# Cross-attention of a perceiver block: denominators of a quarter of the queries from the maximum tiles

## Chip, cores and metric

One core of one Trainium2 chip. The metric is device time in microseconds (us) for one execution, the median of several. Engines are called by the profile's names: PE (TensorE matmul), PEld (TensorE weight load), DVE (VectorE), ACT (ScalarE), POOL (GpSimd), SP (SyncE, which issues the DMAs).

## The reference, cut to what matters

```
q = (x @ Wq + bq).reshape(B, N, 16, 32)        # layer-normed x: 512 queries of 512
k = (y @ Wk + bk).reshape(B, M, 16, 32)        # y: 8192 context rows of 384
v = (y @ Wv + bv).reshape(B, M, 16, 32)
scores = einsum('bnhd,bmhd->bhnm', q, k) / sqrt(32)
attn = softmax(scores, axis=-1)                # over 8192 keys
out = einsum('bhnm,bmhd->bnhd', attn, v).reshape(B, N, 512)
x = x + relu(out @ W1 + b1) @ W2 + b2
x = x + local_attention(layernorm(x))          # 16 heads, window 256
x = x + fp4_ffn(layernorm(x))                  # 1408 inner columns
```

## The kernel before, in words

The program has four stages one after the other: a projection stage (keys, values and queries, and the fp4 quantisation of the FFN's weights), the cross-attention stage, the local attention, and the FFN. The change is in the first two.

**Cross-attention** goes through 16 heads, each in 16 steps q of 512 keys (`QUADS`). A step does, on PE:
- four *maximum tiles* for the head after (`pre`, line 1046; `pre_tile`, line 1038): 128 queries x 512 keys, to find each query's largest score. Their keys are two steps ahead (`AHEAD`), so that in the last two steps of a head they belong to the head after next. They rotate through `PRE_BANKS` = 3 PSUM banks;
- four *score tiles* of this head (`scores`, line 1070): 128 keys x 512 queries, with the maximum already subtracted by an extra row of the stacked queries. They rotate through `S_BANKS` = 3 PSUM banks: a score tile may be written once the exponential three tiles back has been taken (the wait in line 1077; `s_bank`, line 922, has another order for the last four tiles of a head, where the last one goes back two tiles);
- the *denominator*, "den" (`add_to_denominator`, line 1096): a product of a tile of exponentials with a matrix of ones. Of each step's four tiles of exponentials POOL adds up 3 (steps 0, 1 and the odd ones) or 2 (the other even ones) over the head (`add_up`, line 1426); PE multiplies the rest, so one tile or two, two steps late, and at the end of a head the three tiles of POOL's sums (`denominator`, line 1108);
- the *weighted values* of the step before (`weighted`, line 1083), four products of 512 columns in fp32.

Every one of these tiles is four matmuls on the four groups of 32 columns of the array. PE's order within a step is written out by hand, as are all engines' orders:

```
PE_ORDER = ((0,), 0, (1,), 1, "den", 2, (2,), 3, (3,))     # (j,): maximum tile j; t: score tile t
```

and `weighted` behind it. Every engine runs its instructions in its own order and waits at semaphores. ACT takes the exponential of each score tile (line 1261), from PSUM into one of four slots in SBUF. DVE reduces each maximum tile to one column (`tile_max`, line 1294). At the seam between two heads, DVE reduces the maxima to one row (`head_max`, line 1300), PE turns it (`row`, in step 14), ACT copies it into the queries' stack (`copy_row`, line 1229, behind the exponentials of step 14). ACT copies the weighted values of the head before out of PSUM behind step 0 (`read_pv`, line 1234), DVE takes the reciprocal of its denominators ahead of step 2's maxima (`invert`, line 1307; PE's den of step 2 waits for it), PE sums its output behind step 5 (`output`, line 1124), and DVE scales it ahead of step 6's (`scale_out`, line 1311). The last head has no maximum tiles to make; there DVE adds two tiles of exponentials (`sum_tiles`, line 1337) and splits weights.

**The projection stage** already makes the maximum tiles of head 0 and the first two steps of head 1 (18 groups of four, `maxima`, lines 646 and 720), and DVE reduces them. It ends with the first head's maximum row; `warm` (line 584) loads ACT's exponential table there.

## Time and profile before

| | |
|---|---|
| median of 3 runs | 1386.45 us (1385.97 to 1388.21) |
| span of the profiled execution | 1383.2 us |
| PE busy | 1332.2 us (96%) |
| DVE busy | 1120.9 us (81%) |
| ACT busy | 806.1 us (58%) |
| POOL busy | 778.7 us (56%) |
| TensorE clock granted over the span | 0.995 |

The span runs from the first to the last instruction. For the profiled execution no time of its own is given beside the span; the median of the runs lies 3.25 us above it, which is what lies around the span. "Busy" says for what share of the time an engine had an instruction in it; matmuls are pipelined and overlap, so a PE that is always busy may still wait a little.

### The profile page before, as it was taken

What the parts mean: (1) busy time and instruction counts of PE and PEld (TensorE: products, weight loads), DVE (VectorE), ACT (ScalarE), POOL (GpSimd) and SP (SyncE); (2) the same over time, 40 slices, a digit from 0 to 9 for tenths busy, and PEclk for the clock granted to TensorE, in tenths of its full rate; (3) what the DMA queues carried; (4) which work ended last, traced back from release to release, by engine and by line L of the source; (5) the groups of instructions that cost most, each with busy time, mean ns of one, the idle gap of its engine ahead of it and who ended that gap; (6) DMA issues with size and microseconds to landing.
All of it is one profiled execution on the core that took longest, in us unless ns stands there. A gap on an engine that the chain in (4) does not pass through costs nothing. (4 is left out here: it accounts for less than half of the span.)

```text
span 1383.2 us, 39979 instructions
## 1 busy us (share of the span) xinstructions
PE 1332.2 (96%) x17098; PEld 702.8 (51%) x17098; DVE 1120.9 (81%) x1786; ACT 806.1 (58%) x1459; POOL 778.7 (56%) x320
## 2 busy tenths in 40 slices
PE   7999999998999999999999999999999999999898
PEld 4444444443555555555555555545555445566454
DVE  5778888887888888888888888888887746578895
ACT  4454444443777777776777776776777841354332
POOL 0322222122899988988998898899889100201121
PEclk9999999999999999999999999999999999999999
DMA  8568777786352122122212112211210030491000
GB/s 265 177 169 231 207 211 211 210 238 177 91 183 69 39 69 67 30 65 67 69 39 68 56 38 69 67 50 57 59 66 31 5 145 1 92 214 41 0 9 23
DMA packets 127799, 137.54 MB, mean 99 GB/s; under 512 B 44995, under 2 KB 108995, under 8 KB 125699
## 3 DMA queue, kind: packets, MB, share of 16 engines
q1 hardware_dynamic: 127622, 134.98, 34.6%
q8 instruction: 135, 2.21, 0.7%
q14 instruction: 42, 0.34, 0.1%
HBM read 75.70 MB, written 44.17 MB: 87 GB/s over the span
## 5 line engine op out<-in xcount | busy, mean ns | idle before, releaser
L1297 DVE TENSOR_REDUCE early<-attend_banks 128x1 f32<-128x512 f32 x952 | 612.4, 685 | 80.8 <-PE attend_banks L1042 75.6
L1261 ACT ACTIVATE attend_prob<-attend_banks 128x512 f32<-128x512 f32 x1024 | 536.0, 599 | 200.8 <-PE attend_banks L1079 198.6
L1439 POOL TENSOR_TENSOR early<-early,attend_prob 128x1024 f32<-128x1024 f32 x210 | 614.5, 2926 | 37.7 <-ACT attend_prob L1261 9.6
L1079 PE MATMUL attend_banks<-early,k_first 97*32 97x512 f16 x2560 | 258.9, 382 | 3.1 <-ACT attend_prob L1261 3.1
L1042 PE MATMUL attend_banks<-k_first,early 96*32 96x512 f16 x2272 | 235.1, 382 | 1.1 <-PEq L285 1.1
L1079 PE MATMUL attend_banks<-early,attend_k_rest 97*32 97x512 f16 x1536 | 154.1, 381 | 2.8 <-ACT attend_prob L1261 2.8
L1042 PE MATMUL attend_banks<-attend_k_rest,early 96*32 96x512 f16 x1536 | 155.8, 380 | 0.0
L1103 PE MATMUL attend_banks<-attend_prob,ones 128*32 128x128 f32 x3048 | 134.3, 272 | 3.6 <-DVE attend_recip L1309 3.6
L1092 PE MATMUL attend_banks<-attend_prob,wkv_area 128*32 128x512 f32 x1024 | 134.1, 592 | 0.0
L1092 PE MATMUL attend_banks<-attend_prob,attend_vh_odd 128*32 128x512 f32 x1024 | 133.6, 592 | 0.0
L503 POOL TENSOR_TENSOR project_w_whole<-project_grid,project_qscale 128x704 f32<-128x704 f32 x24 | 33.3, 1386 | 173.0 <-DVE project_grid L636 173.0
L1103 PEld LDWEIGHTS attend_banks<-attend_prob,ones 128*32 128x32 f32 x3048 | 95.6, 110 | 54.5 <-DVE attend_recip L1309 11.1
L1079 PEld LDWEIGHTS attend_banks<-early,k_first 97*32 97x32 f16 x2560 | 77.3, 97 | 85.6 <-ACT attend_prob L1261 46.6
L1042 PEld LDWEIGHTS attend_banks<-k_first,early 96*32 96x32 f16 x2272 | 71.3, 97 | 58.4 <-issue 34.9
L555 ACT ACTIVATE project_v<-project_v_ps 128x512 f32<-128x512 f32 x64 | 38.1, 597 | 92.1 <-PE project_v_ps L771 92.1
L497 POOL TENSOR_TENSOR project_qn<-early,project_qinv 128x704 f32<-128x704 f32 x24 | 37.9, 1580 | 87.6 <-issue 50.2
L539 ACT ACTIVATE early<-project_k_ps,project_bk 128x512 f32<-128x512 f32 x64 | 44.0, 688 | 63.6 <-PE project_k_ps L752 61.6
L769 PE MATMUL project_v_ps<-project_w_hi,project_yT_hi 128*128 128x512 f16 x192 | 73.9, 385 | 5.7 <-ACT project_v L555 5.7
L1079 PEld LDWEIGHTS attend_banks<-early,attend_k_rest 97*32 97x32 f16 x1536 | 47.0, 96 | 57.8 <-ACT attend_prob L1261 38.1
L752 PE MATMUL project_k_ps<-project_yT_hi,project_w_hi 128*128 128x512 f16 x192 | 72.5, 379 | 2.3 <-ACT project_q_hi L574 1.4
L770 PE MATMUL project_v_ps<-project_w_lo,project_yT_hi 128*128 128x512 f16 x192 | 73.9, 385 | 0.0
L771 PE MATMUL project_v_ps<-project_w_hi,project_yT_lo 128*128 128x512 f16 x192 | 73.7, 384 | 0.0
(220 smaller groups left out, 1823.6 us busy)
## 6 DMA issues: line engine op xcount, KB each, us to landing
v_scratch<-project_v SPq DMA_DIRECT2D x16, 1024.0 KB, 8.9
early<-in_ctx_dram SPq DMA_DIRECT2D x16, 768.0 KB, 6.2
k_first<-k_scratch SPq DMA_DIRECT2D x36, 256.0 KB, 3.5
k_scratch<-project_k_hi SPq DMA_DIRECT2D x64, 128.0 KB, 2.9
k_scratch<-project_k_lo SPq DMA_DIRECT2D x64, 128.0 KB, 3.1
attend_vh_odd<-v_scratch SPq DMA_DIRECT2D x8, 1024.0 KB, 5.0
wkv_area<-v_scratch SPq DMA_DIRECT2D x7, 1024.0 KB, 4.8
attend_k_rest<-k_scratch SPq DMA_DIRECT2D x24, 256.0 KB, 3.5
```

Of the source, the lines that this page charges most:

```text
L539: nc.scalar.activation(kf[:, g % 2], k_ps[:, g % 2], ACT.Identity, bias=bk[:, g:g + 1], scale=1.0 / WSCALE).then_inc(kf_ready, 1)
L752: last = nc.tensor.matmul(k_ps[:, g % 2], (w_lo if p == 2 else w_hi)[:, 0, k, cols], (yT_lo if p == 1 else yT_hi)[:, u, k], start=(k, p) = ...
L769: nc.tensor.matmul(v_ps[:, t % 2], yT_hi[:, u, k, cols], w_hi[:, 1, k], start=k == 0, stop=False)
L770: nc.tensor.matmul(v_ps[:, t % 2], yT_hi[:, u, k, cols], w_lo[:, 1, k], start=False, stop=False)
L771: last = nc.tensor.matmul(v_ps[:, t % 2], yT_lo[:, u, k, cols], w_hi[:, 1, k], start=False, stop=k == CK - 1)
L1042: last = nc.tensor.matmul(pre_ps[c * HD:(c + 1) * HD, bank, :], q_stack[0:KROWS, h, queries], keys_at(s, part * BLK, (part + 1) * BLK)[0:K ...
L1079: last = nc.tensor.matmul(s_ps[c * HD:(c + 1) * HD, s_bank[n], :], key_rows[:, c * HD:(c + 1) * HD], q_stack[0:KROWS + 1, h, :], start=Tru ...
L1092: last = nc.tensor.matmul(pv_ps[t * HD:(t + 1) * HD, :], vh[s][:, BT * q + t, :], prob[:, q % PSLOTS, t, :], start=q == 0, stop=q == QUADS ...
L1103: last = nc.tensor.matmul(den_ps[t * HD:(t + 1) * HD, 0:P], ones[:], prob[:, q % PSLOTS, n, t * P:(t + 1) * P], start=q == 0 and n == summ ...
L1261: nc.scalar.activation(prob[:, q % PSLOTS, t, :], s_ps[:, s_bank[BT * q + t]], ACT.Exp, scale=SCALE).then_inc(p_ready, 1)
L1297: nc.vector.tensor_reduce(part_max[:, s, j, part:part + 1], pre_ps[:, bank], AX.X, ALU.max).then_inc(pre_read, 1)
L1439: nc.gpsimd.tensor_tensor(sums, sums, prob[:, q % PSLOTS, 0:n], ALU.add).then_inc(pool_summed, 1)
```

## The change

Three quarters of the queries of a head keep their denominators as they were. For the last quarter, maximum tile 3, the denominators come from the maximum tile itself: DVE takes its maximum (now written negated), ACT then takes the exponential of the whole tile in place in PSUM, with the negated maximum as bias and with the row sum as a second output (`sum_tile`), one such operation in each step. Once per head, ACT weighs the 16 row sums with the exponential of each part's maximum less the head's (`weigh`, behind step 1), DVE multiplies, adds up and writes the result on a diagonal (`take_share`, three chained operations ahead of step 3's maxima), and PE adds that to the denominators with four matmuls of 32 columns (`add_share`, in den of step 5).

With it: the scale of the scores moves from the exponential into the queries; POOL adds three tiles in every step, of 384 queries each in place of 512, and PE multiplies one tile of 96 columns per group in place of one or two of 128; the queries are stored in another order (`of_block`), so that each group of 32 rows of the denominators has queries of all four tiles; maximum tile 3 moves to the second place of the step, so that PE's order is maximum 0, maximum 3, score 0, score 1, den, score 2, maximum 1, score 3, maximum 2; PE waits for the row sum before it writes to that bank again (ahead of maximum tile 0 of the next step). The projection stage gets the same sums for its 18 groups (`early_sum`, on ACT), PE waits for them before the next group's tile 3, and `warm` goes.

```
-PE_ORDER = ((0,), 0, (1,), 1, "den", 2, (2,), 3, (3,))
+TILE_ORDER = (0, 3, 1, 2)
+PE_ORDER = ((0,), (3,), 0, 1, "den", 2, (1,), 3, (2,))
+SUM_J = TT - 1
+ADDED = SUM_J * P
...
-        part_max = piece([2, TT, QUADS])
+        tile_low = piece([2, TT, QUADS])
+        part_sum = piece([2, QUADS])
+        part_share = piece([QUADS])
+        share = piece([1])
...
+        def of_block(ap, c):
+            return ap.rearrange("p (j c r) -> p c j r", c=P // HD, r=HD)[:, c]
...
+                        if g == (2 if 2 * i + u < NB - 1 else 1) and (2 * i + u - 1, VALUES_3) not in part_at:
+                            early_sum(2 * i + u - 1, VALUES_1)
...
+                def early_sum(b, place):
+                    if (b, place) in part_at:
+                        h, part = part_at[b, place]
+                        act.wait_ge(pre_read, done_before[b, place] + TT)
+                        nc.scalar.activation(pre_ps[:], pre_ps[:], ACT.Exp, bias=tile_low[:, h, SUM_J, part:part + 1],
+                                             accum_out=part_sum[:, h, part:part + 1]).then_inc(pre_summed, 1)
...
-                    nc.scalar.activation(qf[:, g], k_ps[:, g % 2], ACT.Identity, bias=bq[:, g:g + 1]).then_inc(qf_ready, 1)
-                    nc.scalar.activation(q_hi[:, g], k_ps[:, g % 2], ACT.Identity, bias=bq[:, g:g + 1]).then_inc(qhi_ready, 1)
+                    if g == 0:
+                        act.wait_ge(bias_in, 33)
+                    nc.scalar.activation(qf[:, g], k_ps[:, g % 2], ACT.Identity, bias=bq[:, g:g + 1],
+                                         scale=SCALE).then_inc(qf_ready, 1)
+                    nc.scalar.activation(q_hi[:, g], k_ps[:, g % 2], ACT.Identity, bias=bq[:, g:g + 1],
+                                         scale=SCALE).then_inc(qhi_ready, 1)
...
+                            if j == SUM_J:
+                                wait(pe, pre_summed, done_before[b, place] // TT)
...
-            sum_pool = piece([2, POOL_TILES * T])
+            sum_pool = piece([2, POOL_TILES, ADDED])
+            share_diag = piece([P])
...
-            def pool_tiles(q):
-
-                return POOL_TILES if q < 2 or q % 2 else POOL_TILES - 1
...
+            WEIGH_AT, SHARE_AT, SHARE_ADD_AT = 1, 3, 5
...
+                    freed = turns_of_head[n - PRE_BANKS]
+                    if freed not in ("output", "row") and freed[1] == SUM_J:
+                        wait(pe, pre_summed, EARLY_SUMS + QUADS * (h if n >= PRE_BANKS else h - 1) + freed[0] + 1)
...
-                            last = nc.tensor.matmul(den_ps[t * HD:(t + 1) * HD, 0:P], ones[:],
-                                                    prob[:, q % PSLOTS, n, t * P:(t + 1) * P],
+                            last = nc.tensor.matmul(den_ps[t * HD:(t + 1) * HD, 0:P - HD], ones[:],
+                                                    of_block(prob[:, q % PSLOTS, n, 0:ADDED], t),
                                                     start=q == 0 and n == summed_tiles(h, q), stop=False)
...
-                            last = nc.tensor.matmul(den_ps[t * HD:(t + 1) * HD, 0:P], ones[:],
-                                                    sum_pool[:, s, n * T + t * P:n * T + (t + 1) * P],
+                            last = nc.tensor.matmul(den_ps[t * HD:(t + 1) * HD, 0:P - HD], ones[:],
+                                                    of_block(sum_pool[:, s, n], t),
...
+                def add_share(h):
+                    pe.wait_ge(share_steps, 4 * (h + 1))
+                    for t in range(TT):
+                        nc.tensor.matmul(den_ps[t * HD:(t + 1) * HD, P - HD:P], ones[:],
+                                                share_diag[:, t * HD:(t + 1) * HD], start=False, stop=False)
...
+                                if q == SHARE_ADD_AT:
+                                    add_share(h)
...
+                            pe.wait_ge(pre_summed, EARLY_SUMS + tiles_summed(h, n - PRE_BANKS))
...
+                def sum_tile(s, part, tile, bank):
+                    act.wait_ge(pre_read, tile + 1)
+                    nc.scalar.activation(pre_ps[:, bank], pre_ps[:, bank], ACT.Exp,
+                                         bias=tile_low[:, s, SUM_J, part:part + 1],
+                                         accum_out=part_sum[:, s, part:part + 1]).then_inc(pre_summed, 1)
+                def weigh(h, s):
+                    act.wait_ge(max_ready, h + 1)
+                    wait(act, share_steps, 4 * h)
+                    nc.scalar.activation(part_share[:], tile_low[:, s, SUM_J], ACT.Exp, bias=neg_max[:, s, SUM_J:SUM_J + 1],
+                                         scale=-1.0).then_inc(share_steps, 1)
...
-                            nc.scalar.activation(prob[:, q % PSLOTS, t, :], s_ps[:, s_bank[BT * q + t]], ACT.Exp,
-                                                 scale=SCALE).then_inc(p_ready, 1)
+                            nc.scalar.activation(prob[:, q % PSLOTS, t, :], s_ps[:, s_bank[BT * q + t]],
+                                                 ACT.Exp).then_inc(p_ready, 1)
+                            if t == 1 and ahead(q, last):
+                                s_of, part = (1 - s, q + AHEAD) if q < QUADS - AHEAD else (s, q + AHEAD - QUADS)
+                                sum_tile(s_of, part, TILES * h + TT * q + TILE_ORDER.index(SUM_J), turn_of[(q, SUM_J)] % PRE_BANKS)
+                        if q == WEIGH_AT:
+                            weigh(h, s)
...
-                    nc.vector.tensor_reduce(part_max[:, s, j, part:part + 1], pre_ps[:, bank], AX.X,
-                                            ALU.max).then_inc(pre_read, 1)
+                    nc.vector.tensor_reduce(tile_low[:, s, j, part:part + 1], pre_ps[:, bank], AX.X, ALU.max,
+                                            negate=True).then_inc(pre_read, 1)
...
+                def take_share(h, s):
+                    dve.wait_ge(share_steps, 4 * h + 1)
+                    nc.vector.tensor_tensor(part_share[:], part_share[:], part_sum[:, s], ALU.mult).then_inc(share_steps, 1)
+                    dve.wait_ge(share_steps, 4 * h + 2)
+                    nc.vector.tensor_reduce(share[:], part_share[:], AX.X, ALU.add).then_inc(share_steps, 1)
+                    dve.wait_ge(share_steps, 4 * h + 3)
+                    wait(dve, den_ready, h)
+                    nc.vector.tensor_scalar(share_diag[:], ident[:], share[:], None, ALU.mult).then_inc(share_steps, 1)
...
+                        if q == SHARE_AT:
+                            take_share(h, s)
...
-                    n = pool_tiles(q)
-                    sums = sum_pool[:, s, 0:n * T].rearrange("p (n t) -> p n t", n=n)
+                    sums = sum_pool[:, s]
                     if q:
-                        pool.wait_ge(p_ready, BT * Q + n)
+                        pool.wait_ge(p_ready, BT * Q + POOL_TILES)
                     if q == 1:
                         wait(pool, den_ready, 2 * i + s - 1)
-                        nc.gpsimd.tensor_tensor(sums, prob[:, 0, 0:n], prob[:, 1, 0:n],
+                        nc.gpsimd.tensor_tensor(sums, prob[:, 0, 0:POOL_TILES, 0:ADDED], prob[:, 1, 0:POOL_TILES, 0:ADDED],
```

## Rows read from the trace of the kernel before

**Rows 1.** Windows: busy us of each engine, clock, DMA share and GB/s, two stretches.
```profile
100.00:200.00 100.00, 96.31 (x465) 46.60 (x464) 84.18 (x128) 45.72 (x67) 23.71 (x16) 0.98 0.75 214
500.00:700.00 200.00, 198.13 (x3532) 105.29 (x3524) 174.01 (x276) 141.61 (x271) 181.81 (x63) 1.00 0.20 58
```

**Rows 2.** Timeline of one step with one den tile (start us, us, engine, line).
```profile
656.65 0.39 PE L1042 MATMUL attend_banks<-attend_k_rest,early 96*32 96x512 f16 x4
656.87 0.39 PE L1079 MATMUL attend_banks<-early,k_first 97*32 97x512 f16 x4
...
657.10 2.61 DVE L1297 TENSOR_REDUCE early<-attend_banks 128x1 f32<-128x512 f32 x4 [0.23 <-PE attend_banks L1042]
...
657.40 2.07 ACT L1261 ACTIVATE attend_prob<-attend_banks 128x512 f32<-128x512 f32 x4 [0.96 <-PE attend_banks L1079]
...
658.05 0.10 PEld L1079 LDWEIGHTS attend_banks<-early,k_first 97*32 97x32 f16 x4 [0.20 <-ACT attend_prob L1261]
...
658.62 1.04 PE L1092 MATMUL attend_banks<-attend_prob,wkv_area 128*32 128x512 f32 x8
...
659.48 0.40 PE L1042 MATMUL attend_banks<-attend_k_rest,early 96*32 96x512 f16 x4
```

**Rows 3.** Timeline: the output of a head, and weighted values one step later.
```profile
653.38 0.39 PE L1130 MATMUL attend_banks<-wkv_area,fold 128*32 128x128 f32 x8
...
661.66 1.05 PE L1092 MATMUL attend_banks<-attend_prob,wkv_area 128*32 128x512 f32 x8
```

**Rows 4.** Timeline of a step of the last head, which has no maximum tiles.
```profile
1084.31 2.06 ACT L1261 ACTIVATE attend_prob<-attend_banks 128x512 f32<-128x512 f32 x4 [0.20 <-PE attend_banks L1079]
...
1084.95 0.10 PEld L1079 LDWEIGHTS attend_banks<-early,attend_k_rest 97*32 97x32 f16 x4 [0.30 <-ACT attend_prob L1261]
...
1085.18 1.03 PE L1092 MATMUL attend_banks<-attend_prob,attend_vh_odd 128*32 128x512 f32 x8
```

**Rows 5.** Timeline: the seam of two heads, steps 1 and 2.
```profile
639.91 1.03 PE L1092 MATMUL attend_banks<-attend_prob,wkv_area 128*32 128x512 f32 x8
...
640.77 0.83 PE L1119 MATMUL attend_banks<-early,ones 128*32 128x128 f32 x24
...
641.67 0.96 DVE L1309 RECIPROCAL attend_recip<-attend_banks 128x128 f32<-128x128 f32 x1 [0.69 <-PE attend_banks L1119]
...
642.69 0.43 PE L1103 MATMUL attend_banks<-attend_prob,ones 128*32 128x128 f32 x8 [0.22 <-DVE attend_recip L1309]
...
643.80 1.04 PE L1092 MATMUL attend_banks<-attend_prob,wkv_area 128*32 128x512 f32 x8
```

**Rows 6.** Timeline: steps 14 and 15, and the reciprocal one head earlier.
```profile
592.93 0.96 DVE L1309 RECIPROCAL attend_recip<-attend_banks 128x128 f32<-128x128 f32 x1 [0.69 <-PE attend_banks L1119]
...
679.28 1.07 PE L1092 MATMUL attend_banks<-attend_prob,wkv_area 128*32 128x512 f32 x8
...
682.77 1.03 PE L1092 MATMUL attend_banks<-attend_prob,wkv_area 128*32 128x512 f32 x8
```

**Rows 7.** Groups by form: instruction, count | busy us, mean ns | idle before.
```profile
L1439 POOL TENSOR_TENSOR early<-early,attend_prob 128x1536 f32<-128x1536 f32 x105 | 364.9, 3475 | 22.7 <-ACT attend_prob L1261 9.6
...
L1439 POOL TENSOR_TENSOR early<-early,attend_prob 128x1024 f32<-128x1024 f32 x105 | 249.6, 2377 | 15.1
```

**Rows 8.** Timeline of ACT: operations with a column as bias, back to back; the smallest.
```profile
339.85 0.20 ACT L584 ACTIVATE warm<-ident 128x1 f32<-128x1 f32 x1
...
1127.29 0.68 ACT L1289 ACTIVATE attend_hT<-attend_banks,late 128x512 f32<-128x512 f32 x1
1127.86 0.69 ACT L1286 ACTIVATE k_first<-attend_banks,late 128x512 f16<-128x512 f32 x1
```

**Rows 9.** Timeline of DVE: small operations (128 columns; a reduction).
```profile
653.90 0.29 DVE L1316 TENSOR_TENSOR attend_o_out<-attend_banks,attend_recip 128x128 f32<-128x128 f32 x1 [0.31 <-issue]
...
677.39 0.22 DVE L1304 TENSOR_REDUCE early<-early 128x4 f16<-128x64 f32 x1
```

**Rows 10.** Waits: loads of score tiles, for ACT: total us, times, longest.
```profile
PEld attend_banks L1079 <- ACT attend_prob L1261: 84.6, 284, 1.3
```

More of the change, by code:

```diff
@@ L556, in values_out @@
                                              ACT.Copy, scale=1.0 / WSCALE).then_inc(vs_ready, 1)
+                        if t == 0:
+                            early_sum(2 * i + u - 1, VALUES_3)
+                        if t == 2 and (2 * i + u, VALUES_3) in part_at:
+                            early_sum(2 * i + u, VALUES_1)
+                def early_sum(b, place):
[4 more added lines that the diff above has]
+                                             accum_out=part_sum[:, h, part:part + 1]).then_inc(pre_summed, 1)
                 def two_blocks(i):
@@ L582, in _ @@
                 values_out(i, 0, range(2, BT))
+                early_sum(NB - 1, KEYS_2)
                 values_out(i, 1)
-                nc.scalar.activation(warm[:], ident[:, 0:1], ACT.Exp)
+                early_sum(NB - 1, VALUES_2)
                 act.wait_ge(row_ready, 1)
-                nc.scalar.activation(q_stack[KROWS:KROWS + 1, 0, :], pre_ps[KROWS:KROWS + 1, :], ACT.Copy).then_inc(row_set, 1)
+                nc.scalar.activation(q_stack[KROWS:KROWS + 1, 0, :], k_ps[KROWS:KROWS + 1, 1, :], ACT.Copy).then_inc(row_set, 1)
             @block.vector
@@ L650, in maxima @@
                             dve.wait_ge(pre_ready, done_before[b, place] + j + 1)
-                            nc.vector.tensor_reduce(part_max[:, h, j, part:part + 1], pre_bank(j), AX.X,
-                                                    ALU.max).then_inc(pre_read, 1)
+                            nc.vector.tensor_reduce(tile_low[:, h, j, part:part + 1], pre_bank(j), AX.X, ALU.max,
+                                                    negate=True).then_inc(pre_read, 1)
                 STEPS = []
@@ L822, in _ @@
                 for t in range(TT):
-                    last = nc.tensor.matmul(pre_ps[KROWS:KROWS + 1, t * P:(t + 1) * P], neg_max[:, 0, t:t + 1], identh[:],
+                    last = nc.tensor.matmul(k_ps[KROWS:KROWS + 1, 1, t * P:(t + 1) * P], neg_max[:, 0, t:t + 1], identh[:],
                                             start=True, stop=True)
@@ L911, in perceiver @@
             for q in range(QUADS):
-                turns_of_head += [(q, j) for j in range(TT)]
+                turns_of_head += [(q, j) for j in TILE_ORDER]
                 turns_of_head += ["output"] if q == OUTPUT_AT else ["row"] if q == ROW_AT else []
@@ L929, in keys_at, with ahead @@
                 return k_rest[:, lo - CHK:hi - CHK]
-            def pool_tiles(q):
-                return POOL_TILES if q < 2 or q % 2 else POOL_TILES - 1
+            def ahead(q, last):
+                return last >= (1 if q < QUADS - AHEAD else 2)
+            WEIGH_AT, SHARE_AT, SHARE_ADD_AT = 1, 3, 5
             LAST_SUMMED = QUADS - 2
@@ L1130, in output @@
                         last = nc.tensor.matmul(pre_ps[t * HD:(t + 1) * HD, bank, 0:P], fold[:],
-                                                pv_sum[:, s, t * P:(t + 1) * P], start=True, stop=True)
+                                                of_block(pv_sum[:, s], t), start=True, stop=True)
                     last.then_inc(o_ready, 1)
@@ L1143, in head @@
                     for q in range(QUADS):
-                        ahead = last >= (1 if q < QUADS - AHEAD else 2)
                         for step in PE_ORDER:
                             if step == "den":
+                                if q == SHARE_ADD_AT:
+                                    add_share(h)
                                 if q >= 2:
@@ L1152, in head @@
                                 scores(i, s, q, step)
-                            elif ahead:
+                            elif ahead(q, last):
                                 pre(i, s, q, *step)
@@ L1337, in sum_tiles @@
                 def sum_tiles(q):
-                    sums = sum_pool[:, 1, 0:DVE_TILES * T].rearrange("p (n t) -> p n t", n=DVE_TILES)
+                    sums = sum_pool[:, 1, 0:DVE_TILES]
                     if q:
@@ L1344, in sum_tiles @@
                         dve.wait_ge(den_ready, H - 2)
-                        nc.vector.tensor_tensor(sums, prob[:, 0, 0:DVE_TILES], prob[:, 1, 0:DVE_TILES],
+                        nc.vector.tensor_tensor(sums, prob[:, 0, 0:DVE_TILES, 0:ADDED], prob[:, 1, 0:DVE_TILES, 0:ADDED],
                                                 ALU.add).then_inc(dve_summed, 2)
@@ L1348, in sum_tiles @@
                         dve.wait_ge(dve_summed, q)
-                        nc.vector.tensor_tensor(sums, sums, prob[:, q % PSLOTS, 0:DVE_TILES],
+                        nc.vector.tensor_tensor(sums, sums, prob[:, q % PSLOTS, 0:DVE_TILES, 0:ADDED],
                                                 ALU.add).then_inc(dve_summed, 1)
@@ L1378, in head @@
                             scale_out(*before, out_bank)
-                        if last >= (1 if q < QUADS - AHEAD else 2):
+                        if q == SHARE_AT:
+                            take_share(h, s)
+                        if ahead(q, last):
                             s_of, part = (1 - s, q + AHEAD) if q < QUADS - AHEAD else (s, q + AHEAD - QUADS)
-                            for j in range(TT):
-                                tile_max(s_of, part, j, TILES * h + TT * q + j,
+                            for n, j in enumerate(TILE_ORDER):
+                                tile_max(s_of, part, j, TILES * h + TT * q + n,
                                          turn_of[(q, j)] % PRE_BANKS)
@@ L1438, in add_up @@
                         pool.wait_ge(pool_summed, Q)
-                        nc.gpsimd.tensor_tensor(sums, sums, prob[:, q % PSLOTS, 0:n],
+                        nc.gpsimd.tensor_tensor(sums, sums, prob[:, q % PSLOTS, 0:POOL_TILES, 0:ADDED],
                                                 ALU.add).then_inc(pool_summed, 1)
```

27 lines of the change are left out of this document (17 added, 10 removed).

## Prediction, made before the changed kernel was built

> **What bounds the kernel now.** I read the windows first: between 500 and 700 us PE is busy for 198.13 of 200 us, DVE for 174.01, ACT for 141.61, POOL for 181.81, at granted clock 1.00, the higher level of 2.4 GHz [rows 1]. So PE is full in the attention stage and everybody else has room, DVE the least. The timeline then shows what fills PE, step by step. From maximum tile 0 at 656.65 to the weighted values at 658.62 lie nine groups, 1.97 us or 0.219 us each (four maximum tiles, four score tiles, one den tile); the weighted values take 0.86 us until the next step begins at 659.48. That step takes 2.83 us [rows 2]. A step with two den tiles takes 3.04 us (658.62 to 661.66) [rows 2, 3], which prices a den tile at 0.21 to 0.22. Steps 1 to 2 of a head hold the denominators of the head before and a wait for DVE's reciprocal, 3.89 us (639.91 to 643.80) [rows 5]; step 15, with the maximum row and its copy, 3.49 us [rows 6]; step 6 carries the output, 0.22 more [rows 3]. Seven steps of 2.83, six of 3.04, one of 3.89, one of 3.26 and one of 3.49 make 48.7 us, and the reciprocals of two heads lie 48.74 us apart (592.93 and 641.67) [rows 5, 6]. The ledger closes, so I use it for the changed step.
>
> **The row that decides** is a weight load. ACT starts the first exponential 0.53 us after score tile 0 began (656.87 to 657.40), and the load for score tile 3, which reuses that bank, starts at 658.05, marked as waiting for ACT: 1.18 us after score tile 0 [rows 2]. It happens in many steps: 84.6 us over 284 waits [rows 10]. Today it costs nothing, as six groups (score 0, maximum 1, score 1, den, score 2, maximum 2) stand between the two score tiles, 1.31 us. When PE is really held, its matmul starts with the load: in the last head the load is at 1084.95, again 0.64 after the exponential's start, and the weighted values follow one group after score tile 3, at 1085.18, so score tile 3 began at 1084.96 [rows 4]. Least distance between score tiles 0 and 3: 1.18 us.
>
> **The change part by part.**
>
> PE, den. 23 tiles of exponentials per head become 16, and 19 tiles (with the three of POOL's sums) narrow from 128 to 96 columns. Seven tiles x 0.219 = 1.53 us. The narrowing is worth between nothing and a quarter of 0.219 = 0.055 per tile, up to 1.04 us; I take the middle. The Trainium skill, TensorE: Matmul & The Clock Gate, "Wait — 56ns, not 53.3ns?", says that matmuls start no closer than about 25 ns however short; eight of them make a den tile, so by it the tile would cost 0.20 at least and the narrowing be worth some 0.02. No row here has a narrower matmul to test it. Four matmuls of 32 columns for the share: at most one den tile, 0.22 per head, and they stand in den of step 5.
>
> PE, order. The new order puts maximum 3 ahead of score 0 and leaves score 0, score 1, den, score 2, maximum 1 between score tiles 0 and 3: four groups of 0.219 plus den, 1.04 to 1.10 us. That is under 1.18. So a step is: two groups ahead of score 0 (0.44), 1.18, then score 3 and maximum 2 (0.44), weighted values 0.865: **2.925 us in every step, whatever den costs**. The saved matmuls are bought from a stretch that waits for ACT. Against before, the odd steps grow by 0.095 and the even ones shrink by 0.115.
>
> ACT gains one exponential per step, with a column as bias. Two such operations start 0.57 us apart [rows 8], against 0.49 for the plain ones (four end after 2.07, [rows 2]). Row sums as second output: no row has them. The bounds are nothing, and a whole small operation behind it, 0.20 [rows 8]; I take 0.15. ACT then needs 3 x 0.49 + 0.49 + 0.57 + 0.15 = 2.68 of 2.925 us: it fits. The chain for maximum tile 3: DVE starts tile 0's maximum 0.45 after PE [rows 2], each takes 0.65 (2.61 for four) and ends 0.69 after its start, so tile 3's is there at 1.79; ACT, busy with two exponentials until 1.95, ends the sum at 2.64 + 0.15 = 2.79; PE needs the bank 0.055 later, 2.84, and wants it at 2.925. It holds by 0.08 us.
>
> The same chain after something late on DVE. Step 2 begins at 641.43, three den tiles after 640.77, and the reciprocal ends at 642.63, 1.2 us into it [rows 5], so tile 3's maximum is there at 2.5 and the sum at 3.35, where PE wants 3.22: 0.2 lost. In step 3 take_share comes ahead of the maxima: three dependent operations of about 0.2 to 0.29 each [rows 9], with their gaps 0.67 us, and 0.37 lost. Together 0.57 per head. The weigh of ACT (0.2) falls into its slack of 0.25 in step 1.
>
> POOL: 1536 elements take 3475 ns and 1024 take 2377 [rows 7], so 2.14 ns per element, and 1152 take 2.65 us, in every step of 2.925: hidden. DVE in the last head adds 384 columns for 512: cover by ACT's loop, nothing. The scale in the queries is another immediate and column: nothing, 8 operations in the projection stage.
>
> Sum of a head: 13 steps x 2.925 = 38.03; step 2 with den at the wait for the reciprocal 3.22 plus denominators 0.58 = 3.80; step 6 with the output 3.15; step 15 3.49 as before (there score 3 waits for the second exponential); losses 0.57. That is 49.03 against 48.74, **+0.3 us per head**, 15 heads: +4.4 us. The last head has that ACT loop already and no maximum tiles: 0.
>
> Projection: 18 exponentials of 0.7 on ACT, which is busy for 45.72 of 100 us there while PE is for 96.31 [rows 1]; bounds 0 and 18 x 0.2 of PE waiting; I take 1.2 with the row sum at its end, just ahead of the first maximum row.
>
> Total: +5.6 on 1383.2 + 3.25 around it, 1392.0 us. The median of before is the same 1386.45.
>
> **The rivals.**
>
> *The saved matmuls show (faster, 0.30).* If the wait of score tile 3 is shorter than I read, or the losses of 0.57 don't come, PE's own work sets the step. Losses alone away: 48.46 per head, -0.3 x 15 + 1.2 = 1383. PE full in each step: 8 x 0.219 + 0.865 + den 0.164 to 0.219 = 2.78 to 2.84, per head 13 x 0.09 to 0.145 = 1.2 to 1.9 less than 49.03, with the losses away 1.7 to 2.5, net of before 1.4 to 2.2: 1355 to 1366 us. For it: ACT's and POOL's rows leave room. Against it: 1.18 us stands in two places of the trace. With matmuls at the skill's least distance (same section) den stays at 0.20 and this end is 1362; that hangs on the page alone.
>
> *The row sum becomes the wait (slower, 0.27).* Maximum tile 0 of each step is queued behind the sum of the step before, and all of PE behind it. The point is a row sum that costs over 0.23 us beyond the exponential, or as late a start. At 0.3 a step takes 3.0: 16 x 0.07 + 0.15 more losses = 1.3 x 15 = 19 us more, 1411. At 0.4, 3.1: 1435. For it: the margin is 0.08 and DVE, which must deliver first, is the next fullest engine. Against: the smallest ACT operation is 0.20.
>
> *The change doesn't reduce PE's work (0.03)*: if reading 32-column pieces slows the den matmul, nothing moves, as den is inside the 1.18; only the denominators, +0.2 per head, 1395.
>
> **How the numbers follow.** Forecast 0.40: 1392, own range 1385 to 1400. Faster 0.30, slower by the row sum 0.27, rest 0.03. A measurement of this kernel can tell 0.2% (2.8 us) from nothing. Of the forecast's 0.40 some 0.15 lie within 0.2% of before and 0.25 above; of the faster rival 0.03 within. Faster 0.27, same 0.18, slower 0.55. The range of 8 in 10 takes in the first part of each rival: 1364 to 1418.
>
> **What would show it.** A step of 2.9 us in all of steps 7 to 14, odd and even alike; the load of score tile 3 waiting for ACT in nearly every step and starting 1.18 after score tile 0; PE busy less than 99% in the windows; ACT at about 90%; waits of maximum tile 0 for ACT only in steps 3 and 4. Wrong if steps take 2.8 (the wait is not there), or if maximum tile 0 waits for ACT in every step (the sum is longer than 0.15), or if the first score tile of the attention stage comes more than 3 us later.

## Result and the profile after

The changed kernel takes **1426.73 us** (median of 4 runs, 1426.32 to 1427.4), the kernel before 1386.21 on the same chip (1384.79 to 1388.21): the ratio is 1.0295, 95% interval 1.028 to 1.0309. The change costs 40.5 us, against a forecast of 5.6, and lies outside the range. The profiled execution has a span of 1424.7 us, 41.5 more than before.

Three views of the changed kernel. First the windows [rows 1], PE, PEld, DVE, ACT, POOL in this order, then granted clock and DMA:

```profile
500.00:700.00 200.00, 188.33 (x3172) 77.34 (x3165) 175.29 (x275) 175.52 (x388) 154.59 (x59) 1.00 0.19 56
```

PE has fallen from 198 to 188 of 200 us, so its work went down and its waits went up. No other engine is full: ACT is next with 175.5. The waits (engine, what it waited to do, released by: total us, times, longest):

```profile
PEld attend_banks L1079 <- DVE early L1370: 141.5, 182, 2.1
PEld attend_banks L1119 <- ACT attend_prob L1329: 130.3, 269, 1.3
...
PE attend_banks L1079 <- DVE early L1370: 26.5, 15, 1.8
```

The first line is loads of maximum tiles that wait for DVE. In a plain step such a load waits 0.65 us while PE still works on the weighted values, and PE goes on without a pause, so there it costs nothing. The second line is the wait that I had forecast, and answers to [rows 10]. The third is new: PE itself waits for DVE's maxima 15 times, up to 1.8 us each, once per head with maximum tiles. The groups by form (count | busy us, mean ns) name the operation:

```profile
L1387 DVE TENSOR_SCALAR early<-ident,early 128x128 f32<-128x128 f32 x16 | 39.1, 2442 | 0.6
L1384 DVE TENSOR_REDUCE early<-early 128x1 f32<-128x16 f32 x16 | 2.7, 170 | 0.5
L1382 DVE TENSOR_TENSOR early<-early 128x16 f32<-128x16 f32 x16 | 2.6, 164 | 0.0
```

These are the three operations of `take_share`. The third, which writes the share on the diagonal, takes 2.44 us on average. The 0.286 at the least is the last head's, where POOL adds nothing; the median is 2.579. The timeline of one step 3 shows who stands beside it:

```profile
610.05 1.04 PE L1132 MATMUL attend_banks<-attend_prob,attend_vh_odd 128*32 128x512 f32 x8
...
611.19 0.16 DVE L1382 TENSOR_TENSOR early<-early 128x16 f32<-128x16 f32 x1
...
611.38 0.17 DVE L1384 TENSOR_REDUCE early<-early 128x1 f32<-128x16 f32 x1
611.45 2.63 POOL L1522 TENSOR_TENSOR early<-early,attend_prob 128x1152 f32<-128x1152 f32 x1 [1.16 <-ACT attend_prob L1329]
...
611.59 2.58 DVE L1387 TENSOR_SCALAR early<-ident,early 128x128 f32<-128x128 f32 x1
...
614.09 2.47 DVE L1370 TENSOR_REDUCE early<-attend_banks 128x1 f32<-128x512 f32 x4
...
614.82 0.40 PE L1079 MATMUL attend_banks<-k_first,early 96*32 96x512 f16 x4 [1.78 <-DVE early L1370]
...
615.05 1.03 PE L1132 MATMUL attend_banks<-attend_prob,attend_vh_odd 128*32 128x512 f32 x8
```

POOL's addition starts at 611.45 and ends at 614.08; the diagonal, which starts 0.14 later, ends at 614.17. The maxima come behind it, and PE's maximum tile 2 cannot be written: it waits 1.78 us. This step takes 5.00 us (610.05 to 615.05), and the next 3.33, because the four maxima have to be caught up.

**Where the 41.5 us lie.** The reciprocals of the 16 heads (L1307 in the kernel before, L1391 after) come at 397.71, 1031.99 and 1115.81 (those of head 0, head 13 and the last, counted from 0) before and at 402.81, 1069.21 and 1154.48 after. Up to the first it is +5.1, over 13 heads +32.1 (51.26 for 48.79 each), in the next +2.1 and in the last head -0.6: 38.7 in the attention stage. The other 2.8 lie ahead of the FFN's later tiles (its second tile starts at 1342.7 against 1301.0 us, 41.7 later, where the local attention's masks are still only 38.7 later), in code that the change does not touch. Within the first tile PE waits 3.18 us for DVE (`ffn_xq`), for 1.54 before, and the granted clock over the tile is 0.84 (1321.1 to 1342.7) for 0.91 (1282.4 to 1301.0). The first head is dearer than the others by 2.6 us, and its clock is lower in two stretches:

```profile
345.00:350.00 5.00, 4.80 (x44) 1.81 (x44) 3.50 (x6) 4.31 (x11) 0.52 (x1) 0.50 1.06 254
...
355.00:360.00 5.00, 3.19 (x33) 0.84 (x28) 4.28 (x6) 2.51 (x6) 2.34 (x2) 0.79 0.00 0
```

Before it was 0.78 and 1.00 there. The second stretch is right behind PE's wait of 1.81 us in step 3 (357.53); the first lies ahead of any diagonal.

**The plain steps are as forecast, or nearly.** A plain step of the changed kernel, against [rows 2]:

```profile
676.94 0.60 PE L1119 MATMUL attend_banks<-early,k_first 97*32 97x512 f16 x8
...
677.37 0.34 PE L1143 MATMUL attend_banks<-attend_prob,ones 128*32 128x96 f32 x8
...
677.54 0.39 PE L1119 MATMUL attend_banks<-early,k_first 97*32 97x512 f16 x4
...
678.11 0.10 PEld L1119 LDWEIGHTS attend_banks<-early,k_first 97*32 97x32 f16 x4 [0.46 <-ACT attend_prob L1329]
...
678.43 0.67 ACT L1291 ACTIVATE attend_banks<-attend_banks,early 128x512 f32<-128x512 f32 x1
...
679.00 0.21 ACT L1291 ACTIVATION_READ_ACCUMULATOR attend_banks<-attend_banks,early 128x1 f32 x1
679.09 1.09 ACT L1329 ACTIVATE attend_prob<-attend_banks 128x512 f32<-128x512 f32 x2
```

Score tile 0 starts at 676.94, the load of score tile 3 waits for ACT and starts at 678.11: 1.17 us, forecast 1.18. Steps 7 to 14 take 2.91 to 2.92, forecast 2.925 (one step in each of two heads takes 3.2). The row sum shows as an instruction of its own, 0.21 us; the next exponential starts 0.66 after the sum's, against 0.57 without a second output [rows 8], so it costs 0.09 (forecast 0.15). The two exponentials of [rows 8] write to other places, so this price is rough. The den tile of 96 columns takes 0.17 (677.37 to 677.54).

### The profile page after: what moved, and what is told of

Same layout as the page of the kernel before. It is cut to its first block and busy times, and to the rows that moved or that the text cites. A ratio compares the mean times of both kernels' runs of the same rounds, so it can differ in the third digit from the quotient of the medians.

```text
span 1424.7 us, 39341 instructions
## 1 busy us (share of the span) xinstructions
PE 1332.2 (94%) x16386; PEld 613.9 (43%) x16386; DVE 1153.2 (81%) x1835; ACT 972.7 (68%) x1986; POOL 706.5 (50%) x320
## 5 line engine op out<-in xcount | busy, mean ns | idle before, releaser
L1522 POOL TENSOR_TENSOR early<-early,attend_prob 128x1152 f32<-128x1152 f32 x210 | 555.5, 2645 | 116.1 <-ACT attend_prob L1329 115.8
L1329 ACT ACTIVATE attend_prob<-attend_banks 128x512 f32<-128x512 f32 x1024 | 556.6, 605 | 61.4 <-PE attend_banks L1119 56.4
L1119 PE MATMUL attend_banks<-early,k_first 97*32 97x512 f16 x2560 | 225.9, 384 | 8.6 <-ACT attend_prob L1329 8.5
L1079 PE MATMUL attend_banks<-k_first,early 96*32 96x512 f16 x2272 | 201.6, 382 | 15.6 <-DVE early L1370 12.5
L1291 ACT ACTIVATE attend_banks<-attend_banks,early 128x512 f32<-128x512 f32 x238 | 160.5, 674 | 39.3 <-DVE early L1370 39.3
L1079 PE MATMUL attend_banks<-attend_k_rest,early 96*32 96x512 f16 x1536 | 134.3, 382 | 15.7 <-DVE early L1370 14.0
L1119 PE MATMUL attend_banks<-early,attend_k_rest 97*32 97x512 f16 x1536 | 134.9, 382 | 6.2 <-ACT attend_prob L1329 6.0
L1079 PEld LDWEIGHTS attend_banks<-k_first,early 96*32 96x32 f16 x2272 | 60.3, 96 | 98.2 <-DVE early L1370 72.5
L1143 PE MATMUL attend_banks<-attend_prob,ones 128*32 128x96 f32 x2208 | 94.1, 246 | 3.8 <-DVE attend_recip L1391 3.8
L1143 PEld LDWEIGHTS attend_banks<-attend_prob,ones 128*32 128x32 f32 x2208 | 64.3, 109 | 56.9 <-DVE attend_recip L1391 11.2
```

The costliest lines, as they stand in the source:

```text
L1079: last = nc.tensor.matmul(pre_ps[c * HD:(c + 1) * HD, bank, :], q_stack[0:KROWS, h, queries], keys_at(s, part * BLK, (part + 1) * BLK)[0:K ...
L1119: last = nc.tensor.matmul(s_ps[c * HD:(c + 1) * HD, s_bank[n], :], key_rows[:, c * HD:(c + 1) * HD], q_stack[0:KROWS + 1, h, :], start=Tru ...
L1143: last = nc.tensor.matmul(den_ps[t * HD:(t + 1) * HD, 0:P - HD], ones[:], of_block(prob[:, q % PSLOTS, n, 0:ADDED], t), start=q == 0 and n ...
L1291: nc.scalar.activation(pre_ps[:, bank], pre_ps[:, bank], ACT.Exp, bias=tile_low[:, s, SUM_J, part:part + 1], accum_out=part_sum[:, s, part ...
L1329: nc.scalar.activation(prob[:, q % PSLOTS, t, :], s_ps[:, s_bank[BT * q + t]], ACT.Exp).then_inc(p_ready, 1)
L1522: nc.gpsimd.tensor_tensor(sums, sums, prob[:, q % PSLOTS, 0:POOL_TILES, 0:ADDED], ALU.add).then_inc(pool_summed, 1)
```

## The experiments

Two theories stand after the result. **A:** the diagonal waits for POOL's addition, which reads and writes SBUF as it does; this alone costs the 40 us. **B:** the loss belongs to the rest (row sums, order), and the long diagonal only fills time in which DVE had nothing to do. Below A, the order's distance from score tile 0 to 3 sets a plain step.

### 1. No diagonal

The share goes in as PE's weights, each value 32 times, against the columns of the identity; the DVE operation goes away (the semaphore counts change with it).

```
-    nc.tensor.matmul(den_ps[...], ones[:], share_diag[:, t * HD:(t + 1) * HD], ...)
+    nc.tensor.matmul(den_ps[...], share[:].to_broadcast([P, HD]), ident[:, t * HD:(t + 1) * HD], ...)
-    nc.vector.tensor_scalar(share_diag[:], ident[:], share[:], None, ALU.mult)
```

> The changed kernel, but take_share ends with the reduction: the share goes to PE as the weights, a column read 32 times, against columns of the identity, and the operation that wrote the diagonal is gone. Theory A (that operation, 2.58 us where 0.29 was counted, holds up DVE, the row sum and then PE in step 3): step 3 falls from 5.0 us to about 3.1, a head from 51.2 to 49.3 us, 15 heads, so about 1398 us. Theory B (ACT's fuller program and the new order cost the time, and step 3 only shows it): at most a few us, above 1420 us.

Measured: 1388.92 us (10 runs), ratio 1.002 (1.001 to 1.003). From the changed kernel that is 37.8 us less. The last reciprocal comes at 1116.26, 38.2 earlier than in the changed kernel and 0.45 later than before. DVE in step 3 of this kernel, the maxima right behind the two small operations:

```profile
596.34 0.16 DVE L1382 TENSOR_TENSOR early<-early 128x16 f32<-128x16 f32 x1
596.53 0.17 DVE L1385 TENSOR_REDUCE early<-early 128x1 f32<-128x16 f32 x1
596.63 2.54 DVE L1370 TENSOR_REDUCE early<-attend_banks 128x1 f32<-128x512 f32 x4
```

Step 3 takes 3.03 and step 4 2.91. The time is 9 us below the 1398 that I had put for theory A, as step 4 gets its part of the loss back too and head 0 its clock. Theory B, above 1420 us, is out: the diagonal is what costs. That POOL is the cause is not shown by this run; experiment 4 tests it.

### 2. The new order in the kernel before

```
-PE_ORDER = ((0,), 0, (1,), 1, "den", 2, (2,), 3, (3,))
+PE_ORDER = ((0,), (1,), 0, 1, "den", 2, (2,), 3, (3,))
```

> The kernel before with one thing of the change: maximum tile 1 moved ahead of score tile 0, so that four groups and den stand between score tiles 0 and 3 where five and den stood. Nothing else of the change is in it. Theory (score tile 3 can't start sooner than 1.18 us after score tile 0): steps with one den tile grow from 2.83 to 2.92 us, those with two stay at 3.04 to 3.06, a head by 0.7 to 0.9, so 1397 to 1400 us, with the load of score tile 3 waiting for ACT in every step of one den tile. Rival (the order is free, as PE's own work sets the step): 1386 us.

Measured: 1395.58 us, ratio 1.0069 (1.0049 to 1.009). Its timeline, score tile 0 at 549.92 and score tile 3 at 551.10:

```profile
549.92 0.61 PE L1079 MATMUL attend_banks<-early,k_first 97*32 97x512 f16 x8
...
551.10 0.40 PE L1079 MATMUL attend_banks<-early,k_first 97*32 97x512 f16 x4
```

1.18 us, with a full den tile, no row sum and no share. Steps with one den tile take 2.91 to 2.92, for 2.83. The time is just under the expected 1397 to 1400. So the loop over ACT and its 1.18 us are real, and an order that leaves only four groups and den between the two score tiles costs some 9.7 us by itself. Here the changed kernel buys its saved matmuls back.

### 3. The changed kernel with the distance of before

```
-PE_ORDER = ((0,), (3,), 0, 1, "den", 2, (1,), 3, (2,))
+PE_ORDER = ((0,), 0, (3,), 1, "den", 2, (1,), 3, (2,))
```

> The changed kernel with PE's order maximum 0, score 0, maximum 3, score 1, den, score 2, maximum 1, score 3, maximum 2: five groups and den between score tiles 0 and 3. Theory (that distance sets the step of 2.915 us): steps 7 to 14 fall to 2.78 to 2.80 us, a head by 1.4 to 1.8, so 1400 to 1406 us. Rival (the chain maximum tile 3, DVE, row sum, bank free sets the step): steps stay at 2.9 us or fall by less than 0.05, and maximum tile 0 waits for ACT: 1415 us or more.

Measured: 1420.78 us, ratio 1.0251 (1.0235 to 1.0266); only 6 less than the changed kernel, where 20 to 27 less were expected. Plain steps do take 2.775 us, as expected, and maximum tile 0 does not wait in them, so the rival's mechanism is out, though the time is where it had put it. But in 11 of the 15 heads step 4 takes 4.2 to 5.0 us in place of 3.2. The reason is in the windows around steps 3 and 4 (the figure behind POOL's is the granted clock) and in PE's wait between them. Head 5, counted from 0:

```profile
603.60:608.60 5.00, 3.08 (x52) 1.19 (x48) 4.93 (x8) 2.75 (x6) 2.88 (x2) 1.00 0.00 0
608.60:613.20 4.60, 4.47 (x53) 1.83 (x49) 3.10 (x6) 3.73 (x9) 2.63 (x1) 0.63 0.24 66
```

```profile
608.38 0.40 PE L1079 MATMUL attend_banks<-k_first,early 96*32 96x512 f16 x4 [1.92 <-DVE early L1370]
```

PE comes out of a wait of 1.92 us and runs the next step largely at the lower level (1.2 GHz): two groups of matmuls are 0.42 us apart, at 610.26 and 610.68, for 0.22. Head 10 has the same wait, and its clock stays:

```profile
866.13:870.73 4.60, 4.36 (x72) 1.86 (x68) 4.16 (x8) 4.25 (x10) 2.76 (x2) 1.00 0.23 60
```

```profile
865.90 0.40 PE L1079 MATMUL attend_banks<-attend_k_rest,early 96*32 96x512 f16 x4 [1.92 <-DVE early L1370]
```

Heads 7, 10 and 13, whose clock stays, take 49.6 to 49.7 us, 1.55 less than in the changed kernel, which in 15 heads would be 23 us. The other 11 heads lose 22 us in steps 4 and 5 against that (four of them take 4.2 us in step 5 as well). The order does what was expected of it, and the clock gives most of it away. The length of the wait does not decide it: it is 1.90 to 1.92 us in 14 heads, of which four keep 1.00, and head 14 falls to 0.60 after 1.72, where the changed kernel keeps 1.00 after 1.78. In the 5 us ahead of step 3 heads 5 and 10 have the same rows, too (PE busy 4.66 us, 100 matmuls). What decides stays open.

### 4. POOL's addition cut short, the diagonal kept

In step 2 of each head that POOL adds up, it adds only 16 columns of its 1152, so that it is done before take_share. This leaves most of that step's exponentials out of the denominators.

```
+    elif q == 2:
+        pool.wait_ge(pool_summed, Q)
+        nc.gpsimd.tensor_tensor(sums[:, 0, 0:16], sums[:, 0, 0:16], prob[:, q % PSLOTS, 0, 0:16],
+                                ALU.add).then_inc(pool_summed, 1)
```

> The changed kernel, but POOL's addition of step 2 is cut to 16 columns in each head, so that these exponentials are missing from the denominators; the diagonal is written as in the change. Theory (the diagonal's 2.58 us are a wait for POOL's addition that began 0.14 us before it; in the last head, with POOL idle, it took 0.29): it takes 0.29 us in each head and step 3 falls to about 3.1 to 3.2 us: 1397 to 1402 us. Rival (the operation is slow by itself, its scalar being a column): it stays at 2.4 us and the time at 1427.

Measured: 1387.81 us (one run), 39 less than the changed kernel and 9 below the expected range, for the same reason as in experiment 1. All 16 diagonals (duration in ns, least/median/largest):

```profile
L1387 DVE TENSOR_SCALAR early<-ident,early x16: 285/286/287, 352.4 to 1085.4; 128x128 f32<-128x128 f32 x16
```

The same instruction with the same operands takes 0.286 us when POOL is idle and 2.58 when POOL started just before it. The rival, an operation that is slow by itself, is out. With experiment 1 this settles A: either the diagonal or the addition beside it may be taken away, and the 38 us go. B would have left them. What in SBUF the two engines share, the runs do not tell.

### 5. Both edits, 1 and 3

> The changed kernel with both edits: the share as PE's weights in place of the written diagonal, and maximum tile 3 behind score tile 0. Theory (each step has two limits, PE's own work of 2.78 us and 1.18 us from score tile 0 to 3, and once per head the wait for POOL): steps 7 to 14 take 2.78 us, step 3 about 3.0, the clock stays at its higher level behind it, a head takes 47.2 us against 48.74 before, so 1363 us (1358 to 1370). Rival (ACT, nearly full, gives the rest of its waits back, or the clock falls again in each head): 1378 us or more.

Measured: **1360.53 us** (1358.96 to 1363.21), ratio 0.9826 (0.9813 to 0.984). It is faster than both kernels. Its windows show ACT as the next limit (fourth figure):

```profile
500.00:600.00 100.00, 98.10 (x1736) 48.88 (x1732) 89.86 (x148) 96.45 (x211) 84.68 (x33) 1.00 0.19 56
```

Plain steps take 2.77 to 2.78, steps 3 and 4 2.88 and 2.77. PE's own work is what sets them now: the distance from score tile 0 to 3 is five groups and den. So the whole change is worth about 25 us, if the order leaves the saved denominators free and nothing stands beside POOL.

In head 0 of this run the small product meets the tail of an addition, from 349.34 to 351.99, with 0.22 to 0.23 us of it left:

```profile
349.34 2.65 POOL L1516 TENSOR_TENSOR early<-attend_prob 128x1152 f32<-128x1152 f32 x1 [11.75 <-ACT attend_prob L1329]
...
351.76 0.26 DVE L1382 TENSOR_TENSOR early<-early 128x16 f32<-128x16 f32 x1
```

It takes 0.26 us for 0.165. In experiment 8 the same product takes 0.37 with 0.33 left, and in experiment 6 it takes 2.52 with 2.48 left: each time it ends 0.03 to 0.04 us behind POOL's addition. The price is what is left of the neighbour's instruction.

### 6. Row sums cut to 16 of 512 columns, on top of 5

This leaves out most of the row sum, hence most of that quarter's denominators.

```
-    nc.scalar.activation(pre_ps[:, bank], pre_ps[:, bank], ACT.Exp,
+    nc.scalar.activation(pre_ps[:, bank, 0:16], pre_ps[:, bank, 0:16], ACT.Exp,
```

> As the run with both edits, but the row sums on ACT cover 16 columns of 512, so that most of that share of the denominators is missing; it prices the sums. Theory (in the steady steps they are hidden, at the seams ACT's copies come later by one exponential): step 15 back from 3.86 to 3.49 us, step 1 from 3.08 to 2.8, step 3 to 2.8, steps 7 to 14 unchanged at 2.78: 0.8 us per head, about 12 us less than with both edits, 1351 us. Rival (the sums cost PE nothing in step 15): less than 4 us.

Measured: 1382.95 us (one run), slower by 22 than experiment 5, where 1351 was expected: a miss. Steps 15 and 1 fell as expected (3.50 and 2.77), but step 3 rose to 4.73 in 14 heads, and in four of them (3, 7, 10 and 14, counted from 0) step 4 to 4.44, at a granted clock of 0.61. The timeline of its step 3:

```profile
592.38 2.63 POOL L1520 TENSOR_TENSOR early<-early,attend_prob 128x1152 f32<-128x1152 f32 x1 [1.19 <-ACT attend_prob L1329]
...
592.53 2.52 DVE L1382 TENSOR_TENSOR early<-early 128x16 f32<-128x16 f32 x1
...
595.08 0.17 DVE L1385 TENSOR_REDUCE early<-early 128x1 f32<-128x16 f32 x1
595.16 1.28 DVE L1370 TENSOR_REDUCE early<-attend_banks 128x1 f32<-128x512 f32 x2
```

Now it is the first operation of take_share, 16 columns wide, that takes 2.52 us for 0.16. POOL's addition now starts 0.15 before it. In the changed kernel it started 0.26 ahead of POOL's (611.19 and 611.45), and was over before POOL began. The waits of PE that follow are 1.76 to 1.77 us in heads 1 to 13, the three with the lower clock among them, so here too the length of the wait does not decide.

### 7. The two cuts together

Experiment 6 with the short addition of experiment 4.

> The kernel with the row sums cut to 16 columns, and beside that GpSimd's addition in step 2 of each head cut to 16 columns, as in the run before where only that was cut. It leaves out part of the denominators, as those two do. Theory: in the run with the short row sums the 1382.95 us came from take_share's product of two SBUF tiles of 16 columns (L1382), which took 2.52 us since GpSimd's addition in step 2 had started 0.15 us before it. With that addition short the product takes 0.17, step 3 falls from 4.73 to about 2.9, and the time to 1382.95 - 16 x 1.8 = 1354 (1348 to 1360). Rival: the short row sums make the product late or long by themselves (a wait of DVE for the weighing on ScalarE, or a later start); then it stays at 2.5 us, or step 3 above 4 us, and the time within 1377 to 1385.

Measured: 1349.95 us (one run), 33 less than experiment 6. All 16 of the small products are short again:

```profile
L1382 DVE TENSOR_TENSOR early<-early x16: 163/167/168, 351.3 to 1046.6; 128x16 f32<-128x16 f32 x16
```

So the miss of experiment 6 has the cause of the changed kernel, with another operation as its victim. The expected range was 1348 to 1360. Against experiment 5 the short row sums and the short additions together are worth 10.6 us (on two chips, and from one run here). That is about what a cheaper row sum could still give: steps 15 and 1 shrink by 0.35 and 0.30, which is 9 us in 14 heads.

### 8. The share later in the head

Experiment 5 with `WEIGH_AT, SHARE_AT, SHARE_ADD_AT = 6, 8, 9` for 1, 3, 5, so that the work leaves the steps behind the seam.

> As the run with both edits, with weigh behind step 6, take_share ahead of step 8 and add_share in den of step 9, where neither the reciprocal nor the seam's copies are near. Theory (the small operations of take_share delay the row sum by what DVE has not yet caught up after the reciprocal): step 3 falls from about 3.0 to 2.8 us and step 8 grows by less, 0.1 to 0.2 us per head, 2 to 3 us less in all. Rival (the delay moves with them): the same time within 1 us.

Measured: 1360.32 us (1359.62 to 1360.61), ratio 0.9816 (0.9803 to 0.9829): no difference from experiment 5, as the rival said. Step 3 stays at 2.88 without take_share, so take_share cost nothing there, and step 8 takes 2.77 with it. The 2.84 that step 5 took with add_share stands in step 9 now, and step 7, behind `weigh`, takes 2.84 too. That step 3 still catches up from the reciprocal is my reading; it was not tested.

## Why the prediction was wrong, point by point

**The step that failed** is the last term of the losses: "three dependent operations of about 0.2 to 0.29 each [rows 9], with their gaps 0.67 us, and 0.37 lost". The first two took 0.16 and 0.17. The third took 2.58, and the loss of steps 3 and 4 together came to 2.08 + 0.41 over 2.92, which is 2.5 per head for 0.37. Experiment 1 keeps 0.11 of it, so the diagonal costs 2.39 x 15 = 36 us; the first head's lower clock, which experiment 1 does not have (0.82 and 1.00 in the two stretches), makes up the rest of its 38. What took the price's place is a wait for POOL, which the forecast had called hidden. The first paragraph had already misread the row that matters: "everybody else has room, DVE the least". POOL, with 181.81 of 200 us, had less room than DVE with 174.01 [rows 1].

Why the price looked safe: the row of 0.29 us [rows 9] does lie beside a busy POOL, as this line of the kernel before shows (one line is three additions, 647.06 to 656.68):

```profile
647.06 9.62 POOL L1439 TENSOR_TENSOR early<-early,attend_prob 128x1536 f32<-128x1536 f32 x3 [0.69 <-ACT attend_prob L1261]
```

but it reads PSUM and one tile of SBUF, not SBUF alone. The same width is not the same operands. Beside busy additions of POOL, the attention stage of before with maximum tiles has DVE operations of three kinds: from PSUM, one from PSUM and SBUF, and a reduction with one SBUF input. It had no two-input or scaling operation on SBUF, so I bounded the price by the nearest row and gave no upper end.

The trace of before did hold the price, in the FFN: a scaling from SBUF to SBUF, alone and right behind the start of a subtraction of POOL, six times as long.

```profile
1287.00 0.18 DVE L2134 TENSOR_SCALAR ffn_qscale_f<-ffn_amax_f 128x32 f32<-128x32 f32 x1
...
1369.34 1.16 POOL L2065 TENSOR_TENSOR ffn_hqT<-ffn_whole_T,ffn_hqT 128x512 f16<-128x512 f32 x1 [6.07 <-ACT ffn_whole_T L2093]
1369.37 1.15 DVE L2134 TENSOR_SCALAR ffn_qscale_f<-ffn_amax_f 128x24 f32<-128x24 f32 x1
```

In the projection stage the product L607, with two SBUF inputs, takes 0.68 us at the least and 1.60 at the most, the latter when a POOL product of 1.39 us (L503) began 0.34 earlier (136.57 and 136.91). A list of one line's shortest and longest instruction, over the whole program and not the changed stage alone, would have shown the diagonal's risk before the run.

POOL entered my sum only with its own time ("hidden"), never with what it does to others. The Trainium skill, SBUF — State Buffer, "Who interferes with whom", says just this: a DVE instruction with two SBUF inputs contends with a GpSimd instruction that reads SBUF, tensor_scalar in a two-port mode does so too, and "Whoever issues first gets the shared pair for the whole instruction; the other **fully blocks** (not throttle)". The traces agree for the case in which POOL is first: 2.58 beside and 0.286 without POOL for the diagonal, 2.52 and 0.17 for the small product. Whether the diagonal ran in that mode no trace shows. An estimate by the page, with my 2.65 us for POOL's addition in place of 0.29, would have been 2.36 x 15 = 35 us more than the forecast, 1427.

**The rival that the range names.** "The row sum becomes the wait", 1411 to 1435, holds the number (1426.73) and not the reason, which is luck: PE waits for the row sum only once per head, 0.24 us in step 4, and the sum costs 0.09 and not 0.3. The stated range took in only this rival's first part and ended at 1418.

**What held.**
- The loop from score tile 0 to 3: 1.17 for 1.18, steps of 2.915 for 2.925, odd and even alike; and experiment 2 shows it without the rest of the change.
- POOL: 2.645 us for 2.65, hidden as far as its own time goes.
- The forecast without the diagonal's term (+5.6 less 15 x 0.29, the diagonal's part of the 0.67) would have been about +1.3; experiment 1 measured +3.1 between medians on one chip. In its profile +0.45 lie in the attention stage and 3.4 ahead of the FFN's second tile, so the nearness is in part chance.

**What was off.**
- The narrowing is worth a whole quarter: 0.17 us a den tile for 0.219, so 0.05 (I had taken the middle), which in a waiting step buys nothing. The prediction set this against the Trainium skill, TensorE: Matmul & The Clock Gate, "Wait — 56ns, not 53.3ns?", which puts the least distance of two matmul starts at about 25 ns, and counted that eight times. In the den tile shown above the four matmuls on the four column groups start within 0.01 us of each other, and the tile is two such rounds 0.086 apart, so a floor of 25 ns for each of the eight does not hold here, and the measurement decides. Experiment 5's plain steps of 2.775 need this: 8 x 0.219 + 0.865 + 0.164 = 2.78.
- The seam: I kept step 15 at 3.49 and it takes 3.85; step 1 takes 3.10 and not 2.925. ACT's two copies (the maximum row, the weighted values) now stand behind a row sum; experiment 6 brings them back to 3.50 and 2.77, so it is the row sum. Step 2 took 3.68, for 3.80 and 0.2 of loss: the loss behind the reciprocal did not come.
- The projection stage: +1.2 forecast; the attention's first maximum tile came 0.46 us earlier (342.80 for 343.26), its first score tile 0.24 earlier.

**Open.** The FFN's second tile is late in the profiles of the changed kernel (2.8 us) and of experiment 1 (1304.9 for 1301.0, of which 0.45 come from the attention), and not in those of experiments 2 and 5. In both PE waits 3.2 us for DVE there, where the kernel before and experiments 2 and 5 wait 1.5; experiments 4 and 6 have the long wait too. The clock over the first tile is 0.84 in the changed kernel, but 0.92 in experiment 1 and 0.91 in the others, so the clock alone is not the cause; why was not tried. Nor was the low clock of the changed kernel's first stretch, from 345 to 350 us, nor why the clock falls in some heads of experiments 3 and 6 and stays in others with the same wait. That the winner's small product stays clear of POOL's addition is a matter of tenths of a microsecond in the timing of the steps, as experiment 6 shows; a version in which it cannot collide was not made.

## What to carry to other kernels

Before adding even a tiny DVE operation that scales or combines tiles of SBUF alone, look what GpSimd does at that moment: its price is either its own or the whole remainder of GpSimd's instruction, and tenths of a microsecond in the start decide which. Look for it in the whole trace: one line whose longest instruction is far above its shortest. Price such an operation only by a row with the same kinds of operands beside the same neighbour, and where there is none, take the neighbour's full duration as the upper end. A saved matmul shows only if the order leaves room in the loops through other engines: measure the distance of two tiles that share a bank before moving anything between them.

## What the runs showed of the hardware that was not expected

- A DVE operation of 16 columns with two SBUF inputs: 0.16 to 0.17 us alone, 2.52 when a GpSimd addition of 2.63 started 0.15 earlier. The SBUF-to-SBUF scaling of 128 columns: 0.286 and 2.58. DVE's reductions from PSUM kept their 0.684 on average beside the same additions (0.685 before), and its reductions from SBUF kept 0.170 (16 columns, over the start of an addition) and 0.22 (64 columns, amid one).
- The granted clock can fall after a single wait of PE, and need not: in experiment 3 the same wait of 1.92 us left it at 1.00 over the next step in head 10 and at 0.63 in head 5; in experiment 6 waits of 1.77 left it at 1.00 in ten heads and at 0.61 in three.
- An exponential with a row sum is two instructions on ACT: 0.67 and 0.21 us, of which 0.09 show in the distance to the next one.
- Eight fp32 matmuls of 96 columns, four column groups twice, take 0.17 us; of 128 columns 0.219. The four of a round start within 0.03 us of each other.
